# Windowed attention layers: context with queries as rows, one small-tile stretch a chunk, division after the values, and new engine orders

## The reference

```
a, s = split(x, 2, -1); s shifted by one token           # ahead of both parts
q, k, v = split(x @ Wqkv, 3, -1)                         # 16 heads of 64
q, k = l2norm(q) * qs, l2norm(k) * ksc; rotary with a scale, its inverse for k
windows of 32 tokens: 32 queries see the keys of their own and the previous window, masked to a band
attn = softmax(8 * q @ k.T + mask); out = attn @ v
x = out @ Wo + x
x = (a * gelu(gate)) @ W2 + b2 + x                       # a, gate = layernorm(shifted x) @ W1 + b1
```

## Time and profile before

| | us |
|---|---|
| median of 3 runs | 3864.42 (3851.44 to 3864.74) |
| profiled execution | 3854.79, its span 3853.0 |

### The profile page before, as it was taken

How to read it: one execution, slowest core, us unless ns; L and a number is a source line. 1 busy time by engine, 2 the same in 40 slices (tenths; PEclk the granted TensorE clock), 3 DMA queues, 4 the chain that set the end, 5 groups by cost and what they waited for, 6 DMA issues and landing times. The chain is left out here.

```text
span 3853.0 us, 176449 instructions
## 1 busy us (share of the span) xinstructions
PE 3672.5 (95%) x66944; PEld 2523.9 (66%) x66944; DVE 3196.5 (83%) x6391; ACT 2919.4 (76%) x6003; POOL 3063.6 (80%) x3927
## 2 busy tenths in 40 slices
PE   4999997899999999999999999999999999999997
PEld 2344443567777777777777777777777777777775
DVE  6888884788888888888888888888888888888885
ACT  6466666677777887778777777787778777778874
POOL 5111112989999999999999999999999999999993
PEclk7899999999999999999999999999999999999998
DMA  3433221222222322223222232222232222222222
GB/s 95 61 37 39 39 26 48 79 66 63 64 62 73 83 65 65 65 65 94 65 65 64 63 91 63 64 65 65 71 89 65 65 62 64 73 63 65 65 66 57
DMA packets 179255, 250.64 MB, mean 65 GB/s; under 512 B 46902, under 2 KB 69940, under 8 KB 178228
## 3 DMA queue, kind: packets, MB, share of 16 engines
q1 hardware_dynamic: 179124, 248.92, 26.7%
HBM read 39.07 MB, written 8.39 MB: 12 GB/s over the span
## 5 line engine op out<-in xcount | busy, mean ns | idle before, releaser
L1135 PE MATMUL w_ring<-shared,w_xs 128*128 (+1 forms) x2304 | 1157.3, 605 | 10.0 <-ACT w_xs L1325 4.7
L1540 POOL TENSOR_TENSOR w_qr<-w_raw,w_tc 128x512 f32<-128x512 f32 x384 | 489.0, 1273 | 146.4 <-PE w_ring L1155 138.3
L1554 POOL TENSOR_TENSOR w_qr<-w_qr,w_qrot 128x512 f32<-128x512 f32 x384 | 575.6, 1499 | 0.0
L1135 PEld LDWEIGHTS w_ring<-shared,w_xs 128*128 128x128 f32 x2304 | 378.8, 191 | 176.9 <-issue 143.6
L1547 POOL TENSOR_TENSOR w_qrot<-w_raw,w_tc 128x512 f32<-128x512 f32 x384 | 486.3, 1277 | 0.0
L1217 PEld LDWEIGHTS w_ring<-w_pts,w_vw 64*64 64x64 f32 x24576 | 377.0, 135 | 94.2 <-issue 94.1
L693 ACT ACTIVATE a_probs<-a_wide 128x512 f32<-128x512 f32 (+1 forms) x608 | 314.4, 581 | 156.5 <-PE a_wide L601 154.0
L733 POOL TENSOR_SCALAR_AFFINE_SELECT a_probs<-a_probs 128x512 f32<-128x512 f32 x128 | 81.6, 638 | 441.6 <-ACT a_probs L693 441.6
L764 DVE TENSOR_REDUCE a_row_max<-a_ring 128x1 f32<-128x512 f32 (+3 forms) x608 | 360.9, 654 | 85.2 <-PE a_ring L580 60.4
L1332 ACT ACTIVATE w_ksq<-w_ring 128x512 f32<-128x512 f32 x384 | 229.4, 598 | 251.6 <-PE w_ring L1135 251.6
L1217 PE MATMUL w_ring<-w_pts,w_vw 64*64 64x32 f32 x24576 | 398.6, 220 | 5.2 <-issue 3.5
(11 more groups left out here) (171 smaller groups left out, 8631.0 us busy)
## 6 DMA issues: line engine op xcount, KB each, us to landing
w_vw<-w_v SPq DMA_DIRECT2D x1152, 128.0 KB, 2.3
w_vw<-w_v SPq DMA_DIRECT2D x768, 64.0 KB, 2.0
shared<-in_L_ffn_Wqkv SPq DMA_DIRECT2D x6, 1536.0 KB, 6.0
shared<-q_parts SPq DMA_DIRECT2D x108, 64.0 KB
shared<-k_parts SPq DMA_DIRECT2D x108, 64.0 KB
q_parts<-ap_parts SPq DMA_DIRECT2D x8, 384.0 KB, 4.4
k_parts<-ap_parts SPq DMA_DIRECT2D x8, 384.0 KB, 5.0
shared<-in_L_ffn_Wo SPq DMA_DIRECT2D x12, 256.0 KB, 3.2
```

What stands on the lines that cost most here:

```text
L1135: nc.tensor.matmul(bank(what, i, u)[:], xs[u][:], rhs, start=True, stop=True).then_inc(done, 1)
L1540: nc.gpsimd.tensor_tensor(by_head(qr[i][:]), by_head(raw[i][:]), wide(table(u, Q_COS)), ALU.mult).then_inc(q_straight[i], 1)
L1554: nc.gpsimd.tensor_tensor(qr[i][:], qr[i][:], qrot[i][:], ALU.add).then_inc(q_added[i], 1)
```

## The change

1. values gives the context with queries as rows: the turned probabilities are the stationary operand (64 rows, 32 columns), v the moving one (64 columns).
2. values of one chunk, mask and scores of the next are one function, block(r, u): all its waits first, then values of (r-1, 1) or (r, 0), then mask, then scores of (r, u).
3. divide goes. turn_p takes the exponentials, and normalise_o (DVE) multiplies each context bank by the inverse sums (PSUM to SBUF); turn_o (PE) turns the result back, four transposes a half, into the same bank, from which store_c reads.
4. carry moves from POOL to ACT, and so does the addition of 1e-24 in refine (floored). copy_v writes plainly.
5. The orders of PE, ACT, POOL and DVE and the ring are new. LAG is 4 for 6, and ffn_out of a pair comes one body earlier. In `prepare` one semaphore takes the place of another.

The core of the diff:

```diff
-        rinv = sb("rinv", [P, HEADS])
+        rinv = [sb(f"rinv{u}", [P, HEADS]) for u in range(2)]
+        o = [sb(f"o{par}", [P, 512]) for par in range(2)]
...
-        LAG = 6
...
+        LAG = 4
...
-            def scores(r, u):
...
             def turn_p(r, u, e):
                 if outside(r):
                     return
-                chunk(pe, divided[e], r, u)
+                chunk(pe, exped[e], r, u)
...
-            def values(r, u):
...
-                            for par in range(2):
-                                keys, at = slice(HD * par, HD * (par + 1)), 256 * e + HD * n
-                                out = bank("ct", par, u)
-                                mm = nc.tensor.matmul(out[HD * e:HD * (e + 1), P * n + BAND * w:P * n + BAND * (w + 1)],
-                                                      vw[u][keys, w, at:at + HD], pts[e][keys, n, BAND * w:BAND * (w + 1)],
-                                                      start=True, stop=True)
...
+            def block(r, u):
+
+                rv, uv = (r, 0) if u == 1 else (r - 1, 1)
+                has_scores, has_values = not outside(r), not outside(rv)
+                if not has_scores and not has_values:
...
+                    chunk(pe, carried, r, u)
+                if has_values:
+                    for par in range(2):
+                        chunk(pe, p_stored[par], rv, uv)
+                        wait(pe, v_windows[par][uv], landed)
+                        bank_free(pe, "ct", par, uv, rv)
+
...
+                def score(j):
...
+                def value(n, e):
+                    for w in range(4):
+                        for par in range(2):
+                            rows, keys, at = slice(BAND * w, BAND * (w + 1)), slice(HD * par, HD * (par + 1)), P * n + HD * e
+                            mm = nc.tensor.matmul(bank("ct", par, uv)[rows, at:at + HD], pts[e][keys, n, rows], vw[uv][keys, w, at:at + HD],
+                                                  start=True, stop=True)
+                    return mm
+
+                if has_values:
+                    for n in range(4):
+                        for e in range(2):
+                            vm = value(n, e)
+                    vm.then_inc(valued, 1)
+                if has_scores:
+                    mask()
+                    for j in range(8):
+                        sm = score(j)
+                    sm.then_inc(scored, 1)
+
+            def turn_o(r, u, par):
+                if outside(r):
+                    return
+                chunk(pe, o_ready[par], r, u)
+                out = bank("ct", par, u)
+                for n in range(4):
+                    mm = nc.tensor.transpose(out[:, n * P:(n + 1) * P], o[par][:, n * P:(n + 1) * P], t.ident[:])
+                mm.then_inc(o_flipped[par], 1)
...
-                dst = v[u][:, 512 * i:512 * (i + 1)].rearrange("p (x n d) -> p n x d", x=2, n=4)
-                nc.scalar.copy(dst, bank("v", i, u)[:].rearrange("p (n x d) -> p n x d", n=4, x=2)
-                               ).then_inc(v_copied[i], 1)
+                nc.scalar.copy(v[u][:, 512 * i:512 * (i + 1)], bank("v", i, u)[:]).then_inc(v_copied[i], 1)
...
+                nc.scalar.activation(ssc[:], over[:], ACT.Identity, bias=tiny[:, 0:1]).then_inc(floored, 1)
...
+            def carry(r, u):
+
+                if outside(r):
+                    return
+                for i in range(2):
+                    chunk(act, k_stored[i], r, u, back=1)
+                factor = keep[:, bass.ds(r % PAIRS_B, 1)] if u == 0 else 1.0
+                nc.scalar.activation(kt[u][:, :, 0:BAND], kt[1 - u][:, :, P:KEYS], ACT.Copy, scale=factor).then_inc(carried, 1)
+
...
-                chunk(act, valued, r, u, back=-VALUED_AHEAD)
+                chunk(act, o_flipped[par], r, u)
...
-                nc.gpsimd.tensor_tensor(ssc[:], over[:], tiny[:], ALU.add).then_inc(chain, 1)
+                chunk(pool, floored, r, u)
...
-            def carry(r, u):
...
-                if u == 0:
-                    factor = keep[:, bass.ds(r % PAIRS_B, 1)].unsqueeze(1).broadcast_to([P, HEADS // 2, BAND])
-                    nc.gpsimd.tensor_tensor(kt[u][:, :, 0:BAND], kt[1 - u][:, :, P:KEYS], factor, ALU.mult).then_inc(carried, 1)
-                else:
-                    nc.gpsimd.tensor_copy(kt[u][:, :, 0:BAND], kt[1 - u][:, :, P:KEYS]).then_inc(carried, 1)
...
-            def divide(r, u, e):
-                if outside(r):
-                    return
-                chunk(dve, inverted[e], r, u)
-                nc.vector.tensor_tensor(p[u][e][:], p[u][e][:], per_head(rinv[:, 8 * e:8 * e + 8]), ALU.mult).then_inc(divided[e], 1)
...
+            def normalise_o(r, u, par):
+                if outside(r):
+                    return
+                wait(dve, inverted, 4 * r + 2 * (u + 1))
+                chunk(dve, valued, r, u, back=-VALUED_AHEAD)
+                chunk(dve, o_flipped[par], r, u, back=1)
+                split = "p (n e d) -> p n e d"
+                factor = rinv[u][:].rearrange("p (e n x) -> p x n e", e=2, x=2)[:, par].unsqueeze(3).broadcast_to([P, 4, 2, HD])
+                nc.vector.tensor_tensor(o[par][:].rearrange(split, n=4, e=2), bank("ct", par, u)[:].rearrange(split, n=4, e=2), factor, ALU.mult
+                                        ).then_inc(o_ready[par], 1)
```

More of the change, by code:

```diff
@@ L1464, in body @@
             def body(pair):
-                copy_v(pair - 2, 1, 0)
                 copy_v(pair - 2, 1, 1)
-                store_c(pair - 3, 1, 1)
+                exps(pair - 2, 0, 1)
+                store_qt(pair - 2, 1, 1)
+                store_kt(pair - 2, 1, 1)
                 square_k(pair - 1, 0, 0)
-                store_kt(pair - 2, 1, 1)
-                store_qt(pair - 2, 1, 1)
-                build_xs(pair - 1, 1)
+                store_qt(pair - 2, 1, 0)
                 clamp(pair - 1, 0)
+                store_p(pair - 2, 0, 1)
@@ L1473, in body @@
+                store_kt(pair - 2, 1, 0)
+                build_xf(pair - 3)
+                store_p(pair - 2, 0, 0)
                 factor_log(pair - 1, 0)
-                build_xf(pair - 3)
+                choose_rows(pair - 1)
                 factor_seed(pair - 1, 0)
-                store_kt(pair - 2, 1, 0)
-                store_qt(pair - 2, 1, 0)
+                square_q(pair - 1, 1, 0)
+                copy_q(pair - 1, 1, 0)
                 copy_v(pair - 1, 0, 0)
-                square_q(pair - 1, 1, 0)
@@ L1480, in body @@
-                store_p(pair - 2, 0, 1)
                 var_log(pair - 3)
+                carry(pair - 1, 0)
                 var_seed(pair - 3)
-                copy_q(pair - 1, 1, 0)
+                build_xs(pair, 0)
+                exps(pair - 2, 1, 0)
+                square_k(pair - 1, 1, 1)
                 square_q(pair - 1, 1, 1)
-                store_p(pair - 2, 0, 0)
-                square_k(pair - 1, 1, 1)
-                copy_q(pair - 1, 1, 1)
-                exps(pair - 2, 1, 0)
+                store_c(pair - 2, 0, 1)
@@ L1489, in body @@
+                store_c(pair - 2, 0, 0)
                 scale_xn(pair - 3)
                 copy_v(pair - 1, 0, 1)
-                exps(pair - 2, 1, 1)
-                choose_rows(pair - 1)
-                build_xs(pair, 0)
-                square_k(pair - 1, 1, 0)
-                store_c(pair - 2, 0, 0)
-                store_c(pair - 2, 0, 1)
-                store_kt(pair - 1, 0, 1)
-                gelu(pair - 3, 0)
-                gelu(pair - 3, 1)
-                store_kt(pair - 1, 0, 0)
@@ L1501, in body @@
-                store_qt(pair - 1, 0, 1)
+                copy_q(pair - 1, 1, 1)
+                square_k(pair - 1, 1, 0)
+                store_kt(pair - 1, 0, 0)
+                store_kt(pair - 1, 0, 1)
+                store_qt(pair - 1, 0, 1)
+                clamp(pair - 1, 1)
+                gelu(pair - 3, 1)
+                gelu(pair - 3, 0)
+                exps(pair - 2, 1, 1)
+                factor_log(pair - 1, 1)
                 store_qt(pair - 1, 0, 0)
                 gelu(pair - 3, 2)
-                square_q(pair, 0, 0)
@@ L1505, in body @@
-                clamp(pair - 1, 1)
-                factor_log(pair - 1, 1)
+                store_p(pair - 2, 1, 0)
                 factor_seed(pair - 1, 1)
-                copy_q(pair, 0, 0)
                 store_p(pair - 2, 1, 1)
-                store_p(pair - 2, 1, 0)
-                exps(pair - 1, 0, 0)
-                square_k(pair, 0, 1)
-                exps(pair - 1, 0, 1)
+                carry(pair - 1, 1)
                 square_q(pair, 0, 1)
                 copy_q(pair, 0, 1)
+                square_q(pair, 0, 0)
@@ L1516, in body @@
+                copy_q(pair, 0, 0)
+                copy_v(pair - 1, 1, 0)
+                square_k(pair, 0, 1)
+                exps(pair - 1, 0, 0)
                 store_c(pair - 2, 1, 0)
+                build_xs(pair, 1)
```

(1 more changed line is left out.)

213 lines of the change are left out of this document (102 added, 111 removed), and 12 rows, old and new, of the table USES.

## The result

The changed kernel takes 4335.28 us in the median (4332.97 to 4339.66, 4 runs) where the kernel before takes 3861.21: a ratio of 1.1234 (1.1209 to 1.1258), so 12 per cent slower. The forecast was 4138, with 3960 to 4250 as its range: the direction was right, the time lay outside.

The account below looks back on a forecast made before the run. PE bounded the old pair; the new one was to be bound by a chain of PE 20.4 and ACT 15.1, T = 35.5 us. From 3854.8, 94 pairs add 274, and 9.6 for the median gives 4138 us, range 3960 to 4250.

Parts of the forecast that it names:

- What bounds: PE bounds the old pair at 32.58 us; in the new one the chain through ACT to store_p gives 35.5.
- That is four loads: On ACT, the split gelus need four table loads a pair instead of two; the two added make +2.85 us.
- The chain's parts: PE to ACT's start 20.4 us, then ACT from square_k(1,1) to the end of store_p 15.1: together 35.5.
- PE's part: From the start of block(.,0) through the last projection of k to ACT's start: 20.4 us.
- what lies outside the steady pairs: The smaller LAG and partly filled bodies at the run's ends: 0, within 15 us either way.
- PE's sum: PE's work per pair under the new order: 32.65 us, against 32.58 before.
- the term for entering and leaving: On PE, four small-tile stretches become two, saving 0.2 to 0.56 us a pair; 0.2 taken.
- the mask's saving: In the two block calls, the mask hiding behind values: 0.5 us less each, counted only in a rival.
- Rival (3): In the two block calls the mask hides behind values and loads don't bind: T = 31.65, 3777 us; chance 0.10.
- Values in the shape of scores: On PE, values of a chunk take 1.40 us, as scores do, instead of 2.00: -1.20 a pair.
- Rival (1),: On ACT, each added table load costs twice its 1.30 us: T = 38.1, 4381 us; chance 0.03.
- Rival (2): On ACT, no added loads or hidden ones: T is PE's 32.3 to 32.8, 3838 to 3885 us; chance 0.08.

Follow-up runs that it names:

- e2: The changed kernel with one preload of the table that has both Exp and Ln in front of exps(1,1): 4177.77 us.
- e9: The changed kernel with 16 identity transposes ahead of the wait in turn_p(1,1) and 16 more ahead of the wait in ffn_out: 4297.41 us.
- e5: The changed kernel with exps(1,1) ahead of square_k(1,0), gelus earlier, preload and factor_log behind the last gelu, gate(1) ahead of gate(0): 3820.34 us.
- e7: e5 with square_k(0,0) earlier, add_attention(1) later, and values split from mask and scores by one projection at both places: 3975.03 us.
- e1: The changed kernel with exps(1,1) and factor_log(1) moved from between the gelus to just ahead of gelu(1): 3974.39 us.
- e3: The kernel before with one preload of the Exp and Ln table between gelu(0) and gelu(1), orders as before: 4008.11 us.
- e4: The changed kernel with 16 identity transposes put ahead of the wait for the exponentials in turn_p(1,1): 4328.04 us.

## Why the prediction was right and wrong

- *What bounds.* Right: PE bounded the old pair, ACT's total of 30.1 did not matter, and the chain over square_k(1,1), the gelus and store_p(1,1) bounds the new one. The waits of PE ahead of turn_p(1,1), ffn_out and the first block stand where they were foreseen; the 0.57 ahead of the second was not.
- *The loads.* This is the step that failed: "That is four loads". There are five. I took Exp and Ln as sharing a table because in the earlier trace rows they run without a load between them; but there the load ahead of them is the explicit preload. The load in front of an exps that follows a gelu serves Exp alone. Taking the fifth load out gave 1.7 a pair (e2), of which 1.4 is the longer chain (37.2 against 35.8 us) and 0.3 the clock. With four loads the time was 4178, inside the stated range.
- *The clock.* Left out: no row of before showed PE with waits of this length in the loop, and I let PE's work keep its price. It measured 0.4 a pair (e9). The 157 us of e2 and the 38 us of e9 may not be added, though 4138 and both would give 4333: 0.3 a pair of clock is in both. A mean pair took 37.55 us where I forecast 35.5. The fifth load accounts for 1.4 of these 2.05, the clock for 0.4, and about 0.3 is left, which is the next point.
- *The chain's parts.* ACT was summed as 15.1 and is 16.7 with the fifth load, so 15.4 without. From the end of store_p to the block I put nothing, and it is 0.35. PE's part was 20.4 and is 20.4 in the shown pair (1997.96 to 2018.39), but by luck: 0.57 of a wait and 0.3 of values at the lower clock were added, the pitches of the other work came out 0.3 longer, and the blocks are 1.2 shorter at full clock than the 6.9 I gave them. In the next pair, without the slow values, it is 20.1 (2035.45 to 2055.57). So the chain with four loads would be 20.1 + 15.4 + 0.35 = 35.9, and e2 shows 35.8 to 36.0. Two small terms of the sum beside the chain were off too, in opposite ways: what lies outside the steady pairs had 0 and took about 12 us, and the median of the runs was put 9.6 above the profiled execution and was 1.1 above it.
- *PE's sum.* 32.65 was forecast; e5 shows about 31.6. "By PE alone this is a change without an effect" was wrong: the term for entering and leaving was mis-sized, with 0.2, and the mask's saving was left at nothing; splitting the stretch again lost about 0.9 by the rows of e7. Rival (3), the hidden mask, has the right total of 31.65 and only part of the mechanism, for in e7 the mask alone takes 0.22 and the larger part is the entering and leaving. It had no say as long as ACT's chain was longer. Values in the shape of scores cost what I took, scores' own price.
- *Rival (1),* the loads that cost double: the five switches of the trace lie at 1.29 to 1.30 from start to next start. The Trainium skill, "ScalarE: Activation LUTs", section "What ACT_TABLE_LOAD costs", gives 2.66 us for every switch; this trace shows less than half of that. The Trainium skill, "ScalarE: Activation LUTs", section "Table sets: the hidden batching unit", says to batch activation calls by set. e1 agrees: with exps and factor_log out from between the gelus, two loads are left and three quarters of the loss are gone.
- *Rival (2)* said that the loads might be hidden, for ACT is not full. e3 shows how far that goes: of the 2.85 us that I count for two loads, 1.25 were hidden in the old order.

## What to carry to other kernels

In a pipeline with orders written by hand, an engine that is 80 per cent busy can still be the bound: add up the run of its instructions between the wait that starts it and the store that the next round needs, and put everything that the compiler inserts, such as table loads, at its place in that run. Ask of each inserted load which functions it serves, not how many kinds of function there are. And compare structure and order apart: here the same structure is 12 per cent slower or 0.9 per cent faster than before, by the places of some ten entries.

## What the runs showed of the hardware

- Matmuls of another kind in the same 64*32 tiling run beside those already going: 8 mask matmuls of 512 columns in bf16 cost almost nothing behind 128 small fp32 ones (1.43 us for both in e5, against 0.50 for the mask alone in the earlier trace rows and 0.22 in e7), and the trace records the first of them among the last of the values.
- With waits of PE of 2 us in a pair the granted clock of the loop was 0.95, and four projection instructions behind such a wait took 3.51 us at a clock of 0.52, in place of 1.88 in e4. With two waits filled by transposes of no use it was 1.00. With one filled it was 0.98, and the slow stretch lay behind the other.
- A table load starts when the operation before it has ended and the next operation starts 1.29 to 1.30 us later; a load right behind a preload, as in e3_before_plus_two, costs the same (starts at 2015.82 and 2017.11, the gelu behind them at 2018.40).
